# Linear-attention layers: where the K and Q biases are added, and the order of the engines around it

## What is computed

```python
for i in range(B):                                   # B = 8 layers
    residual = x
    Q = _feature_map(jnp.einsum('nsd,hdk->nshk', x, Wq[i]) + bq[i])   # elu(.) + 1
    Kf = _feature_map(jnp.einsum('nsd,hdk->nshk', x, Wk[i]) + bk[i])
    V = jnp.einsum('nsd,hdk->nshk', x, Wv[i]) + bv[i]
    KV = jnp.sum(Kf * V, axis=1)
    sumK = jnp.sum(Kf, axis=1)
    Z = 1.0 / (Q * sumK[:, None] + 1e-06)
    att = (Q * KV[:, None] * Z).reshape(n, s, H * K)
    y = jax.nn.gelu(att @ Wo[i] + bo[i])
    x = _layer_norm(y + residual, ln1_s[i], ln1_b[i])
    residual = x
    h = jax.nn.gelu(x @ W1[i] + b1[i])
    h = jax.nn.gelu(h @ W2[i] + b2[i])
    x = _layer_norm(h + residual, ln2_s[i], ln2_b[i])
```

## Time and profile before

| | |
|---|---|
| median of 3 runs | 3785.93 us (3782.62 to 3786.3) |
| the profiled execution | 3785.41 us, of which the span of the profile is 3783.7 us |
| busy, share of the span | PE 83%, DVE 75%, ACT 61%, POOL 16% |
| mean granted TensorE clock | 0.917 of 2.4 GHz |
| the stack of layers | from about 1147 us to 3563 us of the span |

### The profile page before, as it was taken

The page is one execution under the profiler, slowest core; times in us unless marked ns, Lnnn a source line. Parts: engine busy times, 40 slices in busy tenths (PEclk is TensorE's granted clock), DMA queues, the critical chain, the costliest instruction groups (busy, mean ns, idle before and its releaser), DMA issues. The chain is left out here.

```text
span 3783.7 us, 53293 instructions
## 1 busy us (share of the span) xinstructions
PE 3158.0 (83%) x15621; PEld 2172.3 (57%) x15621; DVE 2837.6 (75%) x9954; ACT 2301.5 (61%) x3735; POOL 594.3 (16%) x688
## 2 busy tenths in 40 slices
PE   6999999731525999999999999999999999998564
PEld 5777777620513665565566566565665655665243
DVE  4555555538435898898898898888988988998375
ACT  3444444310214787887888788787887878888310
POOL 0000000010631111111111111111211111211122
PEclk9999999955758999999999999999999999999766
DMA  1000000000421000000000000000000000000000
GB/s 48 0 0 0 0 0 0 1 23 0 106 35 57 1 1 23 7 1 23 7 1 23 7 1 23 7 1 18 12 1 18 12 1 1 1 1 1 6 0 23
DMA packets 30486, 46.51 MB, mean 12 GB/s; under 512 B 4152, under 2 KB 20600, under 8 KB 30240
## 3 DMA queue, kind: packets, MB, share of 16 engines
q1 hardware_dynamic: 24608, 39.47, 3.2%
q0 software_dynamic: 5632, 4.20, 0.8%
HBM read 35.17 MB, written 8.49 MB: 12 GB/s over the span
## 5 line engine op out<-in xcount | busy, mean ns | idle before, releaser
L1684 DVE TENSOR_SCALAR t_feat_q<-t_recip,t_neg_mean 128x256 f32<-128x256 f32 x1024 | 393.7, 446 | 137.7 <-ACT t_recip L1540 130.2
L1387 PE MATMUL t_o_ps<-t_feat_q,t_wo 128*128 128x512 f32 x1024 | 479.5, 601 | 14.4 <-issue 11.8
L1532 ACT ACTIVATE t_recip<-t_feat_q,t_z_scale 128x256 f32<-128x256 f32 x1024 | 434.6, 498 | 1.8 <-DVE t_feat_q L1684 1.0
L1518 ACT ACTIVATE t_exp_k<-t_k_ps 128x1024 f32<-128x1024 f32 x256 | 259.9, 1015 | 250.9 <-PE t_k_ps L1364 250.9
L1647 DVE CUSTOM_DVE_ANT_0 t_junk<-t_v_ps,t_feat_k 128x256 f32<-128x256 f32 x1024 | 391.1, 418 | 23.9 <-PE t_v_ps L1364 23.8
L1637 DVE SCALAR_TENSOR_TENSOR t_feat_k<-t_exp_k,t_k_ps 128x256 f32<-128x256 f32 x1024 | 369.1, 416 | 30.5 <-ACT t_exp_k L1518 30.5
L1522 ACT ACTIVATE t_exp_q<-t_q_ps 128x1024 f32<-128x1024 f32 x256 | 261.7, 1022 | 95.3 <-PE t_q_ps L1364 95.0
L1673 DVE SCALAR_TENSOR_TENSOR t_feat_q<-t_exp_q,t_q_ps 128x1024 f32<-128x1024 f32 x256 | 312.7, 1221 | 8.8
L1387 PEld LDWEIGHTS t_o_ps<-t_feat_q,t_wo 128*128 128x128 f32 x1024 | 195.3, 191 | 191.8 <-issue 171.3
L1362 PE MATMUL t_v_ps<-t_x_hi,t_w_hi 128*128 128x512 f32 x512 | 265.3, 518 | 26.8 <-DVE t_w_lo L1628 17.0
L1540 ACT ACTIVATE t_recip<-t_recip 128x1024 f32<-128x1024 f32 x256 | 269.6, 1054 | 2.7
(11 more groups left out here) (348 smaller groups left out, 7488.8 us busy)
## 6 DMA issues: line engine op xcount, KB each, us to landing
t_raw_w<-in_wk SPq DMA_DIRECT2D x8, 512.0 KB, 3.7
t_raw_w<-in_wq SPq DMA_DIRECT2D x8, 512.0 KB, 4.5
t_raw_w<-in_wv SPq DMA_DIRECT2D x8, 512.0 KB, 5.4
t_raw_o<-in_wo SPq DMA_DIRECT2D x8, 512.0 KB, 3.8
t_raw<-in_w SPq DMA_DIRECT2D x16, 256.0 KB, 2.7
x<-in_x SPq DMA_DIRECT2D x4, 512.0 KB, 7.0
tokens_dram<-r_hn SPq DMA_DIRECT2D x8, 256.0 KB, 2.3
e_w_raw<-in_fc_w SPq DMA_DIRECT2D x4, 512.0 KB, 4.3
```

The costliest lines, as they stand in the source:

```text
L1387: last = pe.matmul(o_ps[:], wo[:, chunk, :], feat_q[:, s, chunk, :], start=(chunk == 0), stop=(chunk == NC - 1), skip_group_check=True)
L1518: act.activation(exp_k[:], k_ps[:], ACT.Exp, bias=-1.0).then_inc(c["k_exp"], 1)
L1532: last = act.activation(recip[:, q % 2, k * UNIT + n * SEQ:k * UNIT + (n + 1) * SEQ], feat_q[:, s, chunk, cols], ACT.Ln, bias=1.0, scale=z ...
L1684: last = dve.tensor_scalar(feat_q[:, s, chunk, cols], recip[:, q % 2, k * UNIT + n * SEQ:k * UNIT + (n + 1) * SEQ], -1.0, neg_mean[:, s, n ...
```

## The change

K and Q each get their bias behind their own three passes, from all 128 rows: `three_pass` takes a `bias`, a 128x128 bf16 tile of which rows 0 to 2 hold the three parts and the others are zero, and adds a fourth, full-row bf16 matmul against ones that closes the sum. `biases` and its common wait for K and Q go; `keys` waits for K's tile alone and `queries` for Q's. `raw_b` and `b3` grow from 4 to 16 blocks of 128 columns, filled by one transfer in place of four; the copy L1623 takes 2048 columns in place of 512.

The lists of all engines are written anew. PE makes Q0, K0, Q1, V0 and K1 of unit t+1 at the end of step t (a step -1 is put in front), and the feed-forward of a unit comes one step earlier (t-2 for its first product). ACT, DVE and POOL follow. The takeover of the next layer's weights is spread: biases and Q's and K's weights in steps 6 and 7 of a layer, wo, w1 and w2 by POOL in steps 9 and 11, each with a wait for the last use. `later` leaves waits out for the first units. Around the parts shown, `clip_q` is the first half of the old `feature_q`, and `gelu_y1`, `gelu_y2`, `scale_x1`, `scale_state`, `add_x1`, `add_state` and `split_x1` are the old in-line instructions made into functions, some with one more wait for a tile's last reader. The core of the diff (for the lists only what stands in the new ones):

```diff
-        raw_b = sb("t_raw_b", [P, 4, P], BF16)
+        raw_b = sb("t_raw_b", [P, 2 * NC, P], BF16)
...
-        b3 = sb("t_b3", [P, 4, P], BF16)
+        b3 = sb("t_b3", [P, 2 * NC, P], BF16)
...
         def run(eng, step):
-            for t in range(4):
+            for t in range(-1, 4):
                 step(t, t)
             with eng.Fori(0, LAYERS - 1) as layer:
                 for i in range(4, 12):
-                    step(layer * PER + i, 4 + i, closing=layer + 1 if i == 7 else None, opening=layer + 1 if i == 8 else None)
+                    step(layer * PER + i, 4 + i, layer, i)
             for t in range(UNITS - 4, UNITS + 4):
                 step(t, t)
+        def later(u, n):
+            return not isinstance(u, int) or u >= n
...
-                for kind in range(2):
-                    for half in range(2):
-                        row = 32 * (2 * kind + half)
-                        sp.dma_start(raw_b[row:row + 3, :, :],
-                                     g["bias_dram"][bass.ds(n, 1), :, kind * CH:(kind + 1) * CH]
-                                     .rearrange("a p (q h c) -> (a p) q h c", h=2, c=P)[:, :, half, :]).then_inc(c["raw_b_in"], 16)
+                sp.dma_start(raw_b[0:3, :, :], g["bias_dram"][bass.ds(n, 1), :, :].rearrange("a p (q c) -> (a p) q c", c=P)).then_inc(c["raw_b_in"], 16)
...
-            def biases(t, q):
-                pe.wait_ge(c["k_ready"], 4 * t + q + 1)
-                pe.wait_ge(c["q_ready"], 4 * t + q + 1)
-                for kind, out in ((0, k_ps), (1, q_ps)):
-                    for half in range(2):
-                        rows = slice(32 * (2 * kind + half), 32 * (2 * kind + half) + 3)
-                        pe.matmul(out[:, half * UNIT:(half + 1) * UNIT], b3[rows, q, :], ones_b[rows, :],
-                                  start=True, stop=False, skip_group_check=True)
-            def three_pass(out, kind, chunk, s, first):
+            def three_pass(out, kind, chunk, s, first, bias=None):
                 cols = slice(chunk * P, (chunk + 1) * P)
                 pe.matmul(out, w_hi[:, kind, cols], x_hi[:, s, :], start=first, stop=False, skip_group_check=True)
                 pe.matmul(out, w_hi[:, kind, cols], x_lo[:, s, :], start=False, stop=False, skip_group_check=True)
-                return pe.matmul(out, w_lo[:, kind, cols], x_hi[:, s, :], start=False, stop=True, skip_group_check=True)
+                last = pe.matmul(out, w_lo[:, kind, cols], x_hi[:, s, :], start=False, stop=bias is None, skip_group_check=True)
+                if bias is not None:
+                    last = pe.matmul(out, bias, ones_b[:], start=False, stop=True, skip_group_check=True)
+                return last
             def keys(t, s, q):
+                pe.wait_ge(c["k_ready"], 4 * t + q + 1)
+                if q == 0:
+                    pe.wait_ge(c["b3_ready"], layer_of(t) + 2)
                 for half in range(2):
-                    last = three_pass(k_ps[:, half * UNIT:(half + 1) * UNIT], 0, 2 * q + half, s, False)
+                    last = three_pass(k_ps[:, half * UNIT:(half + 1) * UNIT], 0, 2 * q + half, s, True, b3[:, 2 * q + half, :])
                 last.then_inc(c["k_filled"], 1)
             def queries(t, s, q):
+                pe.wait_ge(c["q_ready"], 4 * t + q + 1)
+                if q == 0:
+                    pe.wait_ge(c["b3_ready"], layer_of(t) + 2)
                 for half in range(2):
-                    last = three_pass(q_ps[:, half * UNIT:(half + 1) * UNIT], 1, 2 * q + half, s, False)
+                    last = three_pass(q_ps[:, half * UNIT:(half + 1) * UNIT], 1, 2 * q + half, s, True, b3[:, NC + 2 * q + half, :])
                 last.then_inc(c["q_filled"], 1)
...
                     pe.wait_ge(c["x1_split"], u + 2)
                     pe.wait_ge(c["w1_ready"], layer_of(u) + 2)
+                elif j == 1:
+                    pe.wait_ge(c["y2_ready"], u + 1)
                 else:
-                    pe.wait_ge(c["hid_ready"], 4 * u + max(j, 1))
+                    pe.wait_ge(c["hid_ready"], 4 * u + j)
...
+            def step(t, at, layer=None, i=None):
                 s, r = at % 2, 1 - at % 2
+                ahead, A, B, C, Dn, E = (active(at, k) for k in range(-1, 5))
+                if A:
+                    queries(t, s, 2)
+                    values(t, s, 1, 0)
+                if E:
+                    pe.wait_ge(c["z2_ready"], t - 4 + 2)
+                    if not isinstance(t, int) or t - 4 + 1 < UNITS:
+                        pe.wait_ge(c["hid_ready"], 4 * (t - 4) + 9)
+                    turn(m0, y2, c["z2_turned"])
                 if C:
+                    pe.wait_ge(c["z1_ready"], t - 2 + 2)
+                    if later(t - 2, 1):
+                        pe.wait_ge(c["hid_ready"], 4 * (t - 2))
+                    turn(m1, y1, c["z1_turned"])
                 if A:
+                    values(t, s, 1, 1)
+                    keys(t, s, 2)
+                    values(t, s, 2, 0)
                 if B:
                     project(t - 1, r, 0)
                 if A:
+                    queries(t, s, 3)
                 if E:
                     pe.wait_ge(c["n2_ready"], 4 * (t - 4) + 5)
                     turn(m0, y2, c["n2_turned"])
                 if A:
+                    keys(t, s, 3)
+                    values(t, s, 2, 1)
                 if Dn:
+                    second_feed_forward(t - 3)
+                if C:
+                    pe.wait_ge(c["n1_ready"], 4 * (t - 2) + 5)
+                    turn(m1, y1, c["n1_turned"])
                 if A:
+                    values(t, s, 3, 0)
+                if B:
+                    project(t - 1, r, 1)
+                if ahead:
+                    pe.wait_ge(c["x_split"], t + 1 + 2)
+                    pe.wait_ge(c["w_ready"], 3 * layer_of(t + 1) + 3)
+                    queries(t + 1, r, 0)
+                    pe.wait_ge(c["x_split"], t + 1 + 2)
+                    pe.wait_ge(c["w_ready"], 3 * layer_of(t + 1) + 2)
+                    keys(t + 1, r, 0)
+                if A:
+                    values(t, s, 3, 1)
+                if B:
+                    project(t - 1, r, 2)
+                if C:
+                    first_feed_forward(t - 2, 0)
+                if ahead:
+                    queries(t + 1, r, 1)
+                    pe.wait_ge(c["x_split"], t + 1 + 2)
+                    pe.wait_ge(c["w_ready"], 3 * layer_of(t + 1) + 4)
+                    values(t + 1, r, 0, 0)
+                    keys(t + 1, r, 1)
+                if C:
+                    first_feed_forward(t - 2, 1)
+                if B:
+                    project(t - 1, r, 3)
+                if ahead:
+                    values(t + 1, r, 0, 1)
+                if C:
+                    first_feed_forward(t - 2, 2)
+                    first_feed_forward(t - 2, 3)
...
+            def step(t, at, layer=None, i=None):
                 s, r = at % 2, 1 - at % 2
+                ahead, A, B, C, Dn, E = (active(at, k) for k in range(-1, 5))
+                if at == -1:
                     act.preload_act_table_set("natural_log_exp_and_others")
                     for k in range(3):
                         swap(0, k)
                 if Dn:
                     first_gelu(t - 3, 2)
+                if C:
+                    gelu_y1(t - 2)
+                if Dn:
                     first_gelu(t - 3, 3)
+                act.preload_act_table_set("natural_log_exp_and_others")
                 if B:
                     log_z(t - 1, r, 1)
                 if A:
                     exp_queries(t, 2)
+                if ahead:
+                    split_x(t + 1, r)
                 if A:
                     exp_keys(t, 2)
                 if B:
                     log_z(t - 1, r, 2)
+                if i == 7:
+                    swap(layer + 1, 1)
+                if E:
+                    scale_state(t - 4)
                 if A:
+                    exp_queries(t, 3)
+                if B:
+                    exp_z(t - 1, 1)
+                if i == 7:
+                    swap(layer + 1, 0)
+                if B:
+                    exp_z(t - 1, 2)
+                if A:
                     exp_keys(t, 3)
+                if Dn:
+                    gelu_y2(t - 3)
+                act.preload_act_table_set("natural_log_exp_and_others")
                 if B:
                     log_z(t - 1, r, 3)
+                if C:
+                    scale_x1(t - 2, s)
+                if ahead:
+                    exp_queries(t + 1, 0)
+                    exp_keys(t + 1, 0)
+                if i == 7:
+                    swap(layer + 1, 2)
+                if A:
+                    log_z(t, s, 0)
+                if B:
+                    exp_z(t - 1, 3)
+                if A:
+                    exp_z(t, 0)
+                if ahead:
+                    exp_queries(t + 1, 1)
+                    exp_keys(t + 1, 1)
```

(89 more changed lines are left out.)

274 lines of the change are left out of this document (62 added, 212 removed).

## The result

The changed kernel takes 3813.65 us (median, 3808.28 to 3815.81) where before takes 3786.11 on the same chip: ratio 1.0066, 95% interval 1.0044 to 1.0088. It is slower, by 25 us by the ratio and by 27.5 between the medians; the forecast was 3768 and faster. The profiled execution of after has a span of 3809.8 us.

The account below looks back on a forecast made before the run. PE was taken as the bound, DVE next. 59 units x 35.5 us + 15 border + 27 slow clock = 2136.5 against 2154.6, so 3768 us, 0.5% less; forecast band 3750 to 3778, range 3740 to 3808.

Parts of the forecast that it names:

- The floor of PE: PE's own work in a steady unit of the changed kernel, laid end to end: 35.3 us, against today's unit of 35.2.
- turning point of 35.8: Steady unit in us at which the change stops winning: (77.8 - 42)/59 = 0.6 above 35.2.
- The waits of the steady unit: PE's waits in the new order: 0.25 us a unit, plus slips of 0 to 0.3; unit taken as 35.5.
- The border step: At each layer's border K's low weights come 2.1 us after PE could start Q0: 7 x 2.1 = 15 us.
- The 27 us of slow clock: Stretches at 1.2 GHz over the 59 units, 1.25% of 2155 us, kept equal before and after.
- Fill and drain: First 4 units and what follows the last: a move of -10 to +10 us, taken as 0.
- The bound of the kernel before: PE bounds the steady unit: 34.05 us of work in 35.2, a margin of only 3%, DVE next.
- the slower one: Rival: new order waits as much as the old, unit 36.4, 59 units 2190, about 3820 us; chance 0.17.
- DVE held beside POOL's split: Slower rival's mechanism: DVE slowed at the clip beside POOL's splits makes Q1 or K3 late; 1.1 us of waits return.
- types cost: Rival: bf16 bias matmuls between fp32r passes lose time at type changes, 16 x 0.3 = 4.8 us a unit, about 4050; chance 0.04.
- The price of a pack by the Trainium skill: Bias group of four at 4 x 0.216/3.07 = 0.28 us; undoing packing would add 2.3 us a unit, not 1.35.

Follow-up runs that it names:

- e10_small_split: e5_pe_unrolled with POOL's split of x1 cut to 8 of 512 columns; 3747.7 us, ratio 0.9930.
- e1_count: Changed kernel with DVE's three splits of the next layer's weights each waiting only for the high half they read; 3776.9 us, ratio 0.9990.
- e9_old_pe_unrolled: Kernel before with PE's loop over the layers written out and nothing else; 3759.1 us, ratio 0.9961.
- e5_pe_unrolled: e1_count with PE's loop over the layers written out, all other engines unchanged; 3759.7 us, ratio 0.9931.
- after_again: The changed kernel once more, unedited, on another chip; 3811.2 us, ratio 1.0062.
- e3_old_nobias: Kernel before without its four groups of 3-row bias matmuls in a unit, waits in front of them kept; 3746.0 us, ratio 0.9909.
- e8_q_first: e5_pe_unrolled with Q0 of a layer's first unit waiting only for Q's low weights, K0 for K's; 3749.5 us, ratio 0.9931.
- e7_pairs: e1_count with K's and Q's biases as eight packs of two 3-row matmuls a unit in place of 16 full-row matmuls; 3800.9 us, ratio 1.0031.

## Why the prediction was wrong

- **The floor of PE was right.** 35.3 us of work in a unit: the passes (84 x 0.2325), fp32 (10.3), transposes (1.75) and 16 x 0.23 make 35.3 in the profile after too. That the sums agree is in part luck: a single bias matmul was put at 0.216 and is 0.23, the upper end of its bounds, 0.2 us a unit, and transposes and passes were put 0.3 too high. The turning point of 35.8 rests on the 42 us of border and clock; with the 65 measured it is 35.4.
- **The waits of the steady unit were mis-sized**: 0.25 in the sum, 0.7 measured. The two that were named are there. The gelu behind K1 holds the feed-forward's third part for 0.26 (forecast 0.15), and V1,1 waits 0.26 for DVE (forecast 0.1). The third is Q1 behind the clip that POOL's split slows, 0.1 to 0.25; it had been allowed 0.0 to 0.3 and was taken as nothing. Even without it floor and waits add up to 35.6, and 35.5 was taken. e10_small_split shows the third cause, worth 0.15; the other two are read from the timeline alone. Together 36.0 in place of 35.5: 59 x 0.5 = 30 us. It is the largest error, and the mechanism was the forecast's.
- **The border step failed**: 15 us in the sum, 7 x 4.8 = 34 measured. "Walked through, K's low weights are ready 2.1 us behind" came true at 1.6 (the wait in e1_count). But the walk let DVE's first split start when Q's high half was there; the code waits for a count that K's must reach. That put 3.46 us of idleness on DVE, and 3.0 us more on the border unit, ahead of PE's transposes and V: 7 x 3.0 = 21 us. e1_count takes it away.
- **The 27 us of slow clock were near by luck.** The 77.8 us of before were split into 51 of border waits and 27 of slow clock, kept as a fixed loss. Border units do make 51 of them, slow clock at the border included, but the other 26 lie in the middle of the layers. 18 of these go with PE's stops at the jump back of its loop and the slow clock beside some of them (e9_old_pe_unrolled takes them off). The profile showed the stops as "issue" with no releaser, and the new order did not remove them. The changed kernel has 30 us there, so the term came out near its size for another cause. e5_pe_unrolled shows that it is no fixed loss: the stops are gone and the clock is 1.00.
- **Fill and drain** moved by -12 and -7 us where 0 was taken (bounds -10 to +10). That of the fill goes with the new order (115 to 118 us in its kernels with biases, 128 in e9_old_pe_unrolled). What follows the last unit varies in one kernel too (344.3 in after, 348.7 in after_again) and is shorter where the granted clock there is higher: 0.77 in after, 0.75 in after_again, 0.73 in before. So the -7 is mostly not the change's.
- **The bound of the kernel before was told too simply.** "PE is therefore the bound" was read from its busy share and its sum of 34.05. Without its packs it stays at 34.6 (e3_old_nobias), so most of their price lay in waits. It did not enter the sum of the new order.
- **Of the rivals**, the slower one came closest: its decision point of 35.8 was passed by 0.2. Its number, 2190 for the 59 units, is the measured 2189.0 by luck: its unit of 36.4 was too long and its 42 us for border and clock too few. DVE held beside POOL's split is a part of the truth (0.15 of the 0.5 that the unit is over the forecast); border and loop make the rest of the error. That types cost is refuted. The price of a pack by the Trainium skill ("TensorE: Matmul & The Clock Gate", section "Part 3: Packing small matmuls"), an estimate of 0.28 for four by its factor of 3.07, did not hold in this place, where two or four took 0.52. That packing pays did hold here for packs of four: 0.52 against 4 x 0.23 = 0.92.

In sum: 2136.5 forecast, + 30 (unit) + 19 (border, 34 for 15) + 3 (middle of the layers, 30 for 27) makes 2189. From there to the whole: 53 us in the 59 units, - 12 (fill) - 7 (behind the last unit) + 11 (late start) make 45 of the 46 us between 3768 and 3813.65.

With both waits mended and PE's loop written out the new order beats both kernels: e8_q_first, 0.9931 (0.9905 to 0.9958). Beside it on the same chip the old order with PE's loop written out has 0.9961 (0.9948 to 0.9975). These intervals overlap, but both hold the scatter of before; compared directly, the four times of e8_q_first (3745.7 to 3751.3) all lie below the ten of e9_old_pe_unrolled (3758.2 to 3766.8). Their profiles are 9 us apart: the new order is 4 shorter in the 59 units (2132.2 against 2136.6) and 13 in the fill (115.1 against 128.4), and in this execution 8 longer ahead of the stack and behind the last unit. The old order with its own border waits mended was not tried.

## What to carry to other kernels

Before an order is costed, check for every wait by count whether the producer makes things in the order in which the consumer counts them: a wait for one too many leaves the result right and cost 26 to 29 us here. Price a matmul not by its length alone but by leaving it out in the old order as well: what stands in waits is cheap there (0.6 of 2.1 us) and dearer in an order that fills them (1.7 of 3.7). Look at waits without a releaser that come once in each turn of a loop: those in the middle of a layer were the jump, and writing the loop out on the busiest engine alone was enough; the one at the border was a count.

## What the runs showed of the hardware

- A pack of 3-row matmuls costs 0.52 us whether it holds two (e7_pairs) or four (before): 0.21 for one stream and 0.3 on entering and leaving. A full-row bf16 matmul of 512 columns between fp32r passes costs 0.23, like these (after).
- The jump back of PE's loop held it for 1.8 to 2.3 us in before and 2.5 to 3.1 in after. Slow clock (1.2 GHz) stood beside some of these stops and not beside others: five of six in after, two of six in e1_count. With the jumps written out (e5_pe_unrolled) the granted clock was 1.00 over 2139 us, though PE stopped for 1.5 us at each border.
- A DVE clip of 128x1024 fp32 takes 0.69 us alone and up to 1.74 beside POOL's split of x1 (after); with that split cut to 8 columns the mean is 0.70 (e10_small_split).
